# A first attention's product with v, cut in two around the step that copies o out

## What is computed

```python
x = x + _L0_attn_ref(_layernorm(x, axis=-1), ...)      # x: (4, 1024, 128)

def _L0_attn_ref(x, ln_gamma, ln_beta, w_qkv, b_qkv, w_out, b_out):
    h = (x - mu) * jax.lax.rsqrt(var + 1e-05) * ln_gamma + ln_beta
    qkv = (h @ w_qkv + b_qkv).reshape(B, T, 3, NUM_HEADS, HEAD_DIM)   # 16 heads of 8
    scores = jnp.einsum('bhqd,bhkd->bhqk', q, k) / np.sqrt(HEAD_DIM)
    attn = jax.nn.softmax(scores, axis=-1)
    out = jnp.einsum('bhqk,bhkd->bhqd', attn, v)
    return residual + out @ w_out + b_out
```

## Time and profile before

| | us |
|---|---|
| median of 3 runs | 2852.88 |
| lowest and highest | 2850.58 and 2855.62 |
| the profiled execution, whole | 2853.52 |
| its span in the profile | 2851.7 |

### The profile page before, as it was taken

One profiled execution on the slowest core, in us unless ns is written; L12 is line 12 of the kernel. 1 busy time (PEld: TensorE's weight loads), 2 busy tenths in 40 slices (PEclk: granted clock), 3 DMA queues, 4 the chain that ended last, 5 costly groups with the idle time before them and its releaser, 6 DMA issues.

```text
span 2851.7 us, 47438 instructions
## 1 busy us (share of the span) xinstructions
PE 2717.7 (95%) x16546; PEld 1818.3 (64%) x16546; DVE 2365.1 (83%) x3996; ACT 1995.7 (70%) x3972; POOL 1065.1 (37%) x1610
## 2 busy tenths in 40 slices
PE   4699999999899999899999999999999999999996
PEld 2122222222588888677777777777777777777774
DVE  7999999997656655777777988889888888888887
ACT  5388988888622232677777777777777776777772
POOL 4200000000300000365555656556556565565561
PEclk9699999999999999999999999999999999999998
DMA  2220000000010000000000000000000000000000
GB/s 68 89 83 24 22 16 24 24 24 2 1 60 1 1 1 1 1 1 1 1 1 1 1 1 1 1 1 3 6 1 1 1 1 9 1 1 1 1 1 16
DMA packets 31038, 35.22 MB, mean 12 GB/s; under 512 B 7656, under 2 KB 18896, under 8 KB 30672
## 3 DMA queue, kind: packets, MB, share of 16 engines
q1 hardware_dynamic: 30800, 32.18, 3.8%
HBM read 23.37 MB, written 8.39 MB: 11 GB/s over the span
## 4 chain that ended last, share of the span: by engine, by line
PE 50%; DVE 7%; issue 2%; ACT 0%; POOL 0%; POOLq 0%; DVEq 0%; ACTq 0%
PE ps L1753 8%; PE ps L1754 7%; PE ps L1758 7%; PE ps L1692 7%; PE ps L1680 7%; DVE neg_maxima L1961 3%; PE ps L1708 2%; PE ps L1710 1%; PE ps L1709 1%; PE ps L1698 1%; PE ps L1697 1%; PE ps L1696 1%; PE ps L1669 1%; PE ps L1670 1%; PE ps L1671 1%
## 5 line engine op out<-in xcount | busy, mean ns | idle before, releaser
L1961 DVE TENSOR_REDUCE neg_maxima<-ps 128x1 f32<-128x1024 f32 x512 | 624.7, 1220 | 147.6 <-PE ps L1758 144.4
L1903 ACT ACTIVATE diff_probs<-ps,neg_maxima 128x1024 f32<-128x1024 f32 x512 | 575.7, 1124 | 92.2 <-DVE neg_maxima L1961 90.5
L692 ACT ACTIVATE probs<-ps 128x512 f32<-128x512 f32 x1024 | 545.3, 601 | 123.6 <-PE ps L758 110.3
L607 DVE TENSOR_REDUCE maxima_of_halves<-ps 128x2 f32<-128x1024 f32 x512 | 586.8, 1219 | 6.0 <-PE ps L712 4.6
L1753 PE MATMUL ps<-z_T_high,y_high 128*128 128x512 f32 x1024 | 464.5, 454 | 5.6 <-ACT diff_probs L1903 5.6
L2235 POOL TENSOR_TENSOR DT_low<-DT_whole,DT_high 128x512 fp32r<-128x512 f32 x256 | 335.0, 1309 | 351.0 <-DVEq L2129 305.4
L1754 PE MATMUL ps<-z_T_low,y_high 128*128 128x512 f32 x1024 | 403.9, 394 | 0.0
L1973 DVE SCALAR_TENSOR_TENSOR D<-diff_probs,ratio 128x1024 f32<-128x1024 f32 x256 | 330.0, 1289 | 9.4 <-DVE ratio L1969 0.4
L712 PE MATMUL ps<-k_stacks,q_stacks 48*128 48x512 bf16 x1024 | 291.8, 403 | 34.3 <-DVE maxima_of_halves L607 26.3
L732 PE MATMUL ps<-probs,v_and_one 128*32 128x512 f32 (+1 forms) x3824 | 320.6, 407 | 0.0
L1758 PE MATMUL ps<-z_T_high,y_low 128*128 128x512 f32 x1024 | 319.4, 393 | 0.0
(11 more groups left out here) (304 smaller groups left out, 4954.6 us busy)
## 6 DMA issues: line engine op xcount, KB each, us to landing
q_stacks<-q_parts_dram SPq DMA_DIRECT2D x192, 32.0 KB
q_parts_dram<-qk_parts SPq DMA_DIRECT2D x12, 256.0 KB, 2.5
k_parts_dram<-qk_parts SPq DMA_DIRECT2D x12, 256.0 KB, 3.5
k_stacks<-k_parts_dram SPq DMA_DIRECT2D x32, 96.0 KB
residual<-in_L_attn_x_dram SPq DMA_DIRECT2D x4, 512.0 KB, 6.1
k_stacks<-k_parts_dram SPq DMA_DIRECT2D x32, 64.0 KB
q_stacks<-neg_max_parts SPq DMA_DIRECT2D x96, 4.0 KB, 1.7
out_dram<-residual SPq DMA_DIRECT2D x3, 512.0 KB, 3.2
```

The source lines that it names most:

```text
L607: nc.vector.tensor_reduce(mx_half[:, own, half, :, p * PB + t, :], ps[:, bank:bank + 2, :], X, ALU.max).then_inc(nat_max, 1)
L692: nc.scalar.activation(probs[:, k % PT, h, :], ps[:, (r + k + i) % S_RING, :], ACT.Exp, scale=SCALE).then_inc(s_free, 1)
L1903: nc.scalar.activation(probs[:, t % 2, m, :], ps[:, 2 * m:2 * m + 2, :].rearrange("p k n -> p (k n)"), ACT.Exp, bias=neg[:, t, m:m + 1], a ...
L1961: nc.vector.tensor_reduce(neg[:, t, m:m + 1], ps[:, 2 * m:2 * m + 2, :].rearrange("p k n -> p (k n)"), X, ALU.max, negate=True).then_inc(m ...
```

## The change

In the late steps the product with v is cut as well. Its first half stands behind i = 3 of the late step, where the whole one stood, ahead of the transposes of o. Its second half stands in the following step (k = 3 or 11) behind i = 0 and its job, ahead of the second score product. The other products with v stay where they are. The late step of units that follow another (k = 2) multiplies block 0 of this unit, so the second half at k = 3 belongs to this unit too.

```diff
--- before.py
+++ after.py
@@ -761,8 +761,13 @@
                             if i != 1:
                                 for j in jobs[i // 2:i // 2 + 1] if i < 3 else jobs[2:]:
                                     scores_by_query((r + n) % RING, j, *turn_of(u, odd, ("max", j)))
-                            part = (True, True) if late and i == 3 else (i == 1, i == 3)
-                            if any(part) and not (late and i == 1):
+                            if late:
+                                part = (i == 3, False)
+                            else:
+                                part = (i == 1, i == 3)
+                            if k % PB == LAG + 1 and i == 0:
+                                products_with_v(u, r, k - 1 - LAG, False, True)
+                            if any(part):
                                 if k >= LAG:
                                     products_with_v(u, r, k - LAG, *part)
                                 elif not starts(u):
```

## The result

The change makes the kernel slower: 2873.26 us against 2853.92 us (medians of four runs each), ratio 1.0071 with a 95% interval of 1.0059 to 1.0083, so 16.8 to 23.7 us. The forecast was 2869.5, or 2870.5 if its 16.6 us are added to this median of before. 2873.26 lies inside the stated range and just above the likeliest case's own, 2862 to 2873.

The account below looks back on a forecast made before the run. VectorE sets the pace. Late steps 9.3 + 4.2 + 2.6 = 16.1 us, with 0.2 for unit 0 and 0.3 for unit 15 16.6; 2853.5 + 16.6 = 2870.1, less 0.6, is 2869.5; range 2856 to 2876.

Parts of the forecast that it names:

- likeliest case: Whole kernel: slower, 2869.5 us, own range 2862 to 2873; chance 0.82 together with its cheaper and dearer forms.
- The wait at o: VectorE's wait for the transposes ahead of the reciprocal at steps 2 and 10: it goes, gaining 0.24 us at step 10.
- job 29: First scores job behind step 10: its bank is held until 339.16, so it can move up by only 0.02 us.
- job 30: Second scores job behind step 10: TensorE's lead is only 0.07 us, so its maximum starts 0.62 us later.
- delay at step 10: Units 0 to 14: 0.62 us each, 9.3 in all; at step 2 of units 1 to 8, 0.53 each, 4.2.
- loss of pairs: Step behind a late one: score products and job no longer overlap in pairs, losing 0.32 + 0.32 - 0.54 = 0.10 us.
- Units 9 to 14: Step 2 there: TensorE can move up near 0.20 us, so the delay is 0.44 each, 2.6 us in all.
- Unit 0: Its step 2, which has no o: cost taken as +0.2 us, bounds -0.4 and +0.65.
- Unit 15: Its two late steps, with no jobs behind: each costs 0 to 0.24 us, 0.3 taken for both.
- dear form: All late steps: 0.7 us everywhere, as when reaction times add up, 20 us, so 2873.
- Faster: Rival, second job behind o: TensorE has slack there, only the gain at o stays, 8.6 us, 2844.3; chance 0.08.
- No change: Rival, late steps: first job moves up the full 0.43 us, only doubled overhead counts, 3.7 us, 2856.6; chance 0.10.

Follow-up runs that it names:

- experiments 4: Maxima over 256 of each 512 columns (short maxima), in the kernel before and in the changed one: 2829.80 and 2843.35 us.
- experiment 5: Changed kernel with the second half behind the next step's first score product but ahead of its job: 2866.86 us, ratio 1.0050 to the kernel before.
- Experiment 3: Changed kernel with only step 10 cut, step 2 keeping the whole product with v: 2865.28 us, ratio 1.0044 to the kernel before.
- experiment 1: Changed kernel with the second half of the late steps' product with v left out altogether: 2848.29 us, ratio 0.9988 to the kernel before.
- experiment 2: Changed kernel with the second half right behind the transposes of o, ahead of the next first score product: 2856.25 us, ratio 1.0011 to the kernel before.
- experiment 6: Changed kernel with the second half behind the second job of the next step: 2867.46 us, ratio 1.0049 to the kernel before.

## Why the prediction was right, point by point

**The wait at o goes, job 29 stays, job 30 is late.** All three as put: the reciprocals' idle fell to 0.9 us (0.0 in the stretch of rows 2), job 29 stands 0.06 behind the end of job 28's maximum, job 30's maximum starts 2.00 behind job 29's. The delay at step 10 was put at 0.62 and is 0.64; at step 2 it was put at 0.53, and the unit of 40.11 leaves 1.20 - 0.64 = 0.56 for it. The forecast unit was about 40.0. The late steps are 17.4 us by these (15 x 0.64 + 14 x 0.56) where 16.1 was forecast, so the mechanism and its size are both right, and not by luck.

**The loss of pairs was right here and too small elsewhere.** The step that named a "loss of pairs" of 0.10 sums 0.32 + 0.57 + 0.32 against 0.54 by rows, so it holds for this kernel. But it took the 0.10 for the whole price of tearing the pair, and that is 0.32, as experiments 4 and 5 show; 0.21 of it was hidden in the wait for the bank. Whoever built on it with the bank free earlier, as the expectation for short maxima did, expected 4.5 to 7.7 us and found 13.6.

**Units 9 to 14.** They were put at 0.44, because job 29 came 0.20 behind its bank there. In the changed kernel the same units show 40.11 like the rest. The 0.20 was no property of these units: in the trace of before they began 0.1 to 0.8 us late, behind the transfer of the shifts, and in the one after that befell units 4 to 7. That term was too small by 6 x 0.12 = 0.7 us.

**Unit 0.** This is the term that was mis-sized: 0.2, with bounds of -0.4 and 0.65, and 1.9, 3.8 and 4.4 us in the three traces with exactly this split there. The prediction counted matmuls at the 2.4 GHz level and left out the clock, which rises just behind this step.

**Unit 15.** Put at 0.3 for two steps. Experiment 3, with step 10 alone cut, shows one of them: of the last two distances between reciprocals one is 0.41 shorter than before and the other 0.64 longer, so a step costs 0.23, near its upper bound of 0.24. In the changed kernel the last two are 0.23 and 0.64 longer. The one ahead of them, with unit 14's last late step in it, is 0.53 shorter (20.42 for 20.95), since in the kernel before its reciprocal had waited for the transposes for 0.88 us.

**The sum.** From unit 0's step 10 to unit 14's, fourteen units took 547.4 us before and 564.9 after: 17.6 by the unrounded starts, of which 14 x 1.20 = 16.8 are the late steps and the rest is the wait for transfers. With 1.9 to 4.4 for unit 0 and 0.3 for the end, 20 to 22 us are explained; the medians lie 19.3 apart, in an interval of 16.8 to 23.7. 16.6 had been forecast, and it is low mainly by unit 0. The prediction's dear form gives 2873, the very time that was measured, but by 0.7 at every late step, which is not what the runs show: that match is luck.

**The rivals.** Faster (2844.3) needed slack at job 30: there is none, and experiment 1 shows that even without the second half it doesn't come. No change (2856.6) needed job 29 to move up: it doesn't; but its price, 0.11 to 0.14 a late step, is real and is what is paid when the second half stands behind the transposes (experiment 2, 2856.25).

**Is there a better place for the second half?** None that was tried beats the kernel before, and by the rows there is little to win: with the second half left out altogether a unit gains 0.15 us, 0.03 of it at step 10. There the place behind the second job costs 0.02, so a kernel that cuts step 10 alone and puts the half there should run as the kernel before. At step 2, where 0.12 could be won, every place that was tried costs more than it gives. That kernel with step 10 alone was not run, and other places at step 3 weren't either.

## What to carry to other kernels

A wait that the profile names on the engine that sets the pace is worth only as much as the next thing behind it can move: ask first which buffer the following job needs and when it is given back. Where two engines are both 97% busy and hand over through two buffers, work of 0.57 us put between two hand-overs cost 0.45 to 0.74 us in most places here (the changed kernel, experiment 5, step 3 of experiment 6). It was nearly free (0.02) in the one place where the engine had a wait for a buffer to fill and no pair was torn, so read such a move step by step and not by the average of a unit. And price a moved matrix product by what it tears apart, not by its own length: products that ran side by side on different rows are paid for one by one when something of another shape comes between them.

## What the runs showed of the hardware

- Score product, job (two products on two row ranges), score product take 0.54 us from the first start to the next work of another kind, and the same 0.53 without the second score product; alone, one such product takes 0.31 to 0.32 (512 columns, 2.4 GHz level).
- A product with v in two parts takes 2 x 0.57 us and in one 1.00: 0.14 for the cut, found again as 0.145 a late step in experiment 2. The Trainium skill, in TensorEngine Tiling (Array Packing), section Key Properties, says that changing the tiling mode drains TensorE. Both prices agree with that; no run parts a drain from another cost of starting a group.
- PE takes up a bank 0.05 to 0.06 us after the end of the maximum that held it (336.95, 341.15, 352.06), and DVE a finished job 0.05 after its end (354.49 behind 353.84 + 0.60).
- The order of a single step at the 1.2 GHz level decided when the clock rose to 2.4 GHz: 8.9 to 10.8 us behind unit 0's first score product with the product with v whole or its halves together (six traces), 12.8 to 19.8 with them split around the next score product or the second left out (six traces). In the three traces with exactly the change's split and full maxima, unit 0 took 1.9 to 4.4 us longer up to its reciprocal.
